# A mixture-of-experts kernel on one core: every expert's split weights get a place of their own in SBUF

## The reference

```python
x = x + jnp.tanh(g_xattn[0]) * _L0_xattn_ref(_layernorm(x), ctx_2048, ...)   # 16 heads of 8 channels, 8 sequences
x = x + jnp.tanh(g_ffn[0]) * _L0_ffn_ref(_layernorm(x), ...)
...
# _L0_ffn_ref: H = 256, M = 176, E = 32 experts, TOPK = 6, 1024 tokens
scores = jax.nn.sigmoid(xf @ w_router)
sfc = scores + corr_bias                       # 4 of 8 groups by their two best, then 6 experts of those
topk_w = jnp.take_along_axis(scores, topk_idx, axis=1)
combine = jnp.zeros((T, E)).at[jnp.arange(T)[:, None], topk_idx].add(topk_w)
eo = jnp.einsum('etm,emh->eth', jax.nn.silu(g) * u, down_w)                   # g, u: xf by gate_w, up_w
routed = jnp.einsum('te,eth->th', combine, eo)
shared = jax.nn.silu(xf @ sh_gate_w) * (xf @ sh_up_w) @ sh_down_w
return routed + shared
```

## Time and profile before

| | |
|---|---|
| median of three runs | 479.46 us |
| profiled execution: span from first to last instruction (no other time is listed for it) | 481.2 us |
| attention and splitting of weights | 0 to about 261 us |
| shared expert, dispatch of rows, table and padding | about 261 to 311 us |
| 79 blocks | about 311 to 463 us |
| sums and output | about 463 to 481 us |
| PE busy | 385.2 us, 80% |
| DVE busy | 353.6 us, 73% |
| ACT busy | 286.4 us, 60% |
| GpSimd busy | 208.0 us, 43% |
| moved by DMA | 101.63 MB, mean 211 GB/s |

### The profile page before, as it was taken

How to read it: one execution, slowest core, us unless ns; L and a number is a source line. 1 busy time by engine, 2 the same in 40 slices (tenths; PEclk the granted TensorE clock), 3 DMA queues, 4 the chain that set the end, 5 groups by cost and what they waited for, 6 DMA issues and landing times.

```text
span 481.2 us, 11851 instructions
## 1 busy us (share of the span) xinstructions
PE 385.2 (80%) x3518; PEld 252.4 (52%) x3518; DVE 353.6 (73%) x998; ACT 286.4 (60%) x538; POOL 208.0 (43%) x368
## 2 busy tenths in 40 slices
PE   0546487987969696958767768899999999999994
PEld 0423244443525253523433445578888888888873
DVE  8157676879998999999746674467777777677784
ACT  1362768687868777865653412366666666666620
POOL 3530102322363656454344650036666566665650
PEclk9996779797979889986857689999999999999999
DMA  7997336563856747676403797577998896545496
GB/s 204 313 308 103 102 101 196 184 206 122 250 170 218 253 154 253 191 238 222 161 29 114 232 311 263 165 238 238 299 287 277 289 291 207 163 151 162 152 378 251
DMA packets 79614, 101.63 MB, mean 211 GB/s; under 512 B 13824, under 2 KB 67808, under 8 KB 79552
## 3 DMA queue, kind: packets, MB, share of 16 engines
q1 hardware_dynamic: 59744, 67.17, 45.1%
q10 hardware_dynamic: 13712, 15.47, 10.6%
q0 software_dynamic: 6096, 18.23, 10.3%
HBM read 56.74 MB, written 44.09 MB: 210 GB/s over the span
## 4 chain that ended last, share of the span: by engine, by line
PE 55%; DVE 24%; DMA 5%; ACT 5%; issue 5%; SPq 2%; ACTq 2%; POOL 0%; PEldq 0%; DVEq 0%; POOLq 0%
PE ps L1183 13%; DVE wide L1287 9%; PE ps L1095 9%; PE ps L990 6%; PE ps L994 5%; DMA ctxb<-picked_rows 4%; PE ps L1165 3%; PE ps L973 3%; DVE rD L1295 3%; DVE pk L1371 3%; PE ps L1087 2%; PE ps L1088 2%; PE ps L930 1%; PE ps L1001 1%; PE ps L959 1%
## 5 line engine op out<-in xcount | busy, mean ns | idle before, releaser
L1287 DVE TENSOR_REDUCE wide<-ps 128x4 f32<-128x1024 f32 x64 | 76.2, 1222 | 24.9 <-PE ps L959 23.9
L690 ACT ACTIVATE wide<-ps 128x1024 f32<-128x1024 f32 x64 | 64.7, 1025 | 36.9 <-PE ps L973 36.4
L1183 PE MATMUL ps<-wide,bxT 128*128 x474 | 83.6, 313 | 0.5 <-ACT bxT L868 0.5
L640 POOL DMA_INDIRECT picked_rows<-by,bid x79 | 77.9, 986 | 12.9 <-POOL tick L639 12.6
L1508 DVE SCALAR_TENSOR_TENSOR bh<-ps,bx,bsg 128x176 f32<-128x176 f32 (+1 forms) x158 | 47.2, 338 | 42.5 <-ACT bsg L884 41.2
L868 ACT ACTIVATE bxT<-ps 128x512 f16<-128x512 f16 x79 | 47.2, 597 | 30.9 <-PE ps L1165 15.6
L1095 PE MATMUL ps<-wide,bhT 112*128 (+1 forms) x395 | 56.5, 272 | 0.3 <-DVE bhT L1517 0.2
L591 POOL DMA_INDIRECT rows_by_expert<-pay,place x48 | 48.4, 1009 | 12.2 <-issue 11.4
L1183 PEld LDWEIGHTS ps<-wide,bxT 128*128 128x128 f16 x474 | 43.1, 98 | 17.0 <-issue 0.8
L990 PE MATMUL ps<-wide 128*32 128x256 f32 x512 | 48.5, 457 | 0.0
L994 PE MATMUL ps<-wide,onesM 128*32 128x256 f32 x512 | 47.0, 444 | 0.0
(11 more groups left out here) (217 smaller groups left out, 738.5 us busy)
## 6 DMA issues: line engine op xcount, KB each, us to landing
bx<-rows_by_expert ACTq DMA_DIRECT2D x72, 160.0 KB
split_weights<-pk SPq DMA_DIRECT2D x26, 352.0 KB, 2.3
wide<-split_weights SPq DMA_DIRECT2D x26, 352.0 KB
raw<-in_L_ffn_gate_w SPq DMA_DIRECT2D x32, 176.0 KB, 2.9
raw<-in_L_ffn_up_w SPq DMA_DIRECT2D x32, 176.0 KB, 2.9
split_weights<-pk SPq DMA_DIRECT2D x26, 192.0 KB, 2.7
wide<-split_weights SPq DMA_DIRECT2D x26, 192.0 KB
rows_by_expert<-filling SPq DMA_DIRECT2D x1, 4960.0 KB, 15.7
```

The source lines that it names most:

```text
L640: nc.gpsimd.indirect_dma_start(PICKED, bass.IndirectOffsetOnAxis(ap=bid[:, j:j + 1], axis=0), by[:, j, :], None).then_inc(placed[j], 16)
L690: act.activation(Pb[:, u % NP, :, :, :], ring(f"B{u}").rearrange("p (i s t) -> p i s t", i=2, s=KT), ACT.Exp, scale=SCALE).then_inc(emptie ...
L1183: last = pe.matmul(ps[:, buf, 0:2 * M], bxT[:, buf, a, k, :], ring_w[:, bass.ds(given[u] + (2 * k + w) * 2 * M, 2 * M)], start=(n == 0), s ...
L1287: dve.tensor_reduce(nmx[:, :, J, 2 * pair:2 * pair + 2, ROW].rearrange("p c g -> p g c"), ring(f"A{u}").rearrange("p (i c s) -> p i c s", ...
```

## The change

- `wide` becomes one room of 32 places, and expert e lies at place e (`all_w`). The ring and its loop are gone. The room of places 9 and up is shared with tiles of the earlier stages: places 9 to 17 with `raw`, `ctxb`, `qk32` and others that are used until the weights are split, 18 to 28 with the heads' tiles, 29 to 31 with those that hold a sequence's rows until they are sent.
- `HELD` is 9: three more experts are never stored or fetched.
- SP fetches each of the other 23 experts in one DMA of 544 KB (L458 of the change). It waits for the expert two before it, by one semaphore for even and one for odd numbers. Experts 9 to 17 wait for the shared expert's split (`w_lo`), 18 to 28 for the end of attention (`p_used`, as 6 to 11 before), and 29 to 31 come after SP's padding.
- The memset of `full` to -1 goes, so an expert without rows has no block. That makes 64 blocks before the fillers, and 15 fillers.
- SP fetches the rows of the first 72 blocks. ACT fetches the last seven.
- The eight parts of the end all lie in `wide`.

The diff, cut:

```diff
-WR = 16
-HELD = 6
-HELD_FIRST = 12
+HELD = 9
+SP_FETCHES = 72
...
+        wide = sb("wide", [128, NE * WX // 2])
+        all_w = wide[:, :].bitcast(F16)
+        with_context = (("raw", RAW * EACH_RAW), ("ctxb", (B + 1) * T), ("xnb", 2 * T), ("qk32", 2 * T), ...
+        with_heads = (("Pb", NP * NG * T), ("qS", NJ * T), ...
+        with_rows = (("rD", T), ("ob", T), ("wT", 4 * 128), ("wo_t", T), ...
+        room, at = {}, HELD * WX // 2
+        free_from = []
+        for group in (with_context, with_heads, with_rows):
+            for name, size in group:
+                room[name] = wide[:, at:at + size]
+                at += size
+            free_from.append(at * 2 // WX)
...
+        parts = [wide[:, six * i:six * (i + 1)] for i in range(B)]
...
+            for par in range(2):
+                sp.sem_inc(weights_in[par], 16 * ((HELD + 1 - par) // 2 + par))
+                sp.wait_ge(stored[par], 32 * ((NE + 1 - par) // 2 - (HELD + 1 - par) // 2))
+
+            def fetch_experts(start, end):
+
+                for e in range(start, end):
+                    sp.wait_ge(weights_in[e % 2], 16 * ((e + 1) // 2))
+                    sp.dma_start(all_w[:, WX * e:WX * (e + 1)], PACK[e]).then_inc(weights_in[e % 2], 16)
+
+            sp.wait_ge(w_lo, 2 * (NE + 2))
+            fetch_experts(HELD, free_from[0])
             sp.wait_ge(p_used, 4 * B)
-            for e in range(HELD, HELD_FIRST):
-                fetch_expert(e, e)
+            fetch_experts(free_from[0], free_from[1])
             sp.wait_ge(tb_step, 1)
             ...
+            sp.wait_ge(pay_step, 3 * B)
+            sp.wait_ge(xT_lo, B)
+            fetch_experts(free_from[1], NE)
             sp.wait_ge(table_ready, 1)
             rows_sent(sp)
-            for b in range(WB - 1):
+            for b in range(SP_FETCHES):
                 row = entry(mybir.EngineType.SP, row_of, b, SPARE + 128 * (SPARES - 1))
-                sp.dma_start(bx[:, b, :], XS[bass.ds(row, 128)]).then_inc(bx_in[b], 16)
-            for e in range(HELD_FIRST, WR):
-                fetch_expert(e, e)
-            with sp.Fori(0, NE // WR - 1) as t:
...
+                if b >= WB:
+                    sp.wait_ge(bid_done, b - WB + 1)
+                sp.dma_start(bx[:, b % WB, :], XS[bass.ds(row, 128)]).then_inc(bx_in[b % WB], 16)
...
-            dve.memset(full[:, :, 0], -1.0)
...
-                dve.tensor_scalar(blocks_to[:, :], tb[0:1, 1, :], 1.0, None, ALU.add)
...
+            dve.tensor_scalar(odd_16[:, :], expert, 16.0, 16.0, ALU.mult, ALU.add).then_inc(odd_step, 1)
+            dve.tensor_scalar(even_of[:, :], even, 16.0, None, ALU.add)
             dve.tensor_copy(row_of[:, :], row)
+            dve.tensor_scalar(place_of[:, 2:130], expert, float(WX), None, ALU.mult)
+            dve.wait_ge(odd_step, 1)
+            dve.tensor_tensor(odd_of[:, :], odd_16[:, :], even, ALU.subtract)
```

More of the change, by code:

```diff
@@ L130, in build @@
[L130 to L136, removed]
@@ new lines, in build @@
+        for group in (with_context, with_heads, with_rows):
[3 more added lines that the diff above has]
+            free_from.append(at * 2 // WX)
+        assert at <= NE * WX // 2
+        raw = room["raw"]
+        ctxb = room["ctxb"].rearrange("p (b t) -> p b t", b=B + 1)
+        xnb = room["xnb"].rearrange("p (a t) -> p a t", a=2)
+        qk32 = room["qk32"].rearrange("p (a t) -> p a t", a=2)
+        qkh, qkl = (room[name].bitcast(F16).rearrange("p (a t) -> p a t", a=2) for name in ("qkh", "qkl"))
@@ new lines, in build @@
+        wnat, wT, onesM = (room[name].rearrange("p (a t) -> p a t", a=4) for name in ("wnat", "wT", "onesM"))
+        ctxv, rD, ob, wo_t, squares, xc, xn2 = (room[name] for name in ("ctxv", "rD", "ob", "wo_t", "squares", "xc", "xn2"))
+        v32, xT32 = (room[name].rearrange("p (k c) -> p k c", k=KT) for name in ("v32", "xT32"))
+        kB = room["kB"].bitcast(F16).rearrange("p (j t) -> p j t", j=NJ)
+        Pb = room["Pb"].rearrange("p (n i s t) -> p n i s t", n=NP, i=2, s=KT)
+        qS, kS, q2S = (room[name].bitcast(F16).rearrange("p (a j t) -> p a j t", a=2, j=NJ) for name in ("qS", "kS", "q2S"))
@@ L204, in split_of @@
             if kind * 4 + i < HELD:
-                whole = ring_w[:, WX * r:WX * (r + 1)]
+                whole = all_w[:, WX * r:WX * (r + 1)]
             else:
@@ L214, in build @@
         six = TOPK * T
-        parts = [raw[:, six * i:six * (i + 1)] for i in range(3)]
-        parts += [pk[:, :, :].rearrange("p b w -> p (b w)").bitcast(F32)[:, 0:six],
-                  wide[:, 0:six], xT_room[:, 0:six], wide[:, six:2 * six], ctxb[:, :, :].rearrange("p b t -> p (b t)")[:, 0:six]]
+        parts = [wide[:, six * i:six * (i + 1)] for i in range(B)]
         bx = sb("bx", [128, WB, PAY])
@@ L861, in keep_xT @@
                     return
-                loads = act.value_load(loads_of[0:1, bass.ds(b, 1)], min_val=16, max_val=16 * NE)
-                act.wait_ge(experts_in, loads)
-                act.wait_ge(downs_in, loads)
+                even = act.value_load(even_of[0:1, bass.ds(b, 1)], min_val=16, max_val=16 * NE // 2)
+                odd = act.value_load(odd_of[0:1, bass.ds(b, 1)], min_val=16, max_val=16 * NE // 2 + 16)
+                act.wait_ge(weights_in[0], even)
+                act.wait_ge(weights_in[1], odd)
                 act.wait_ge(bxT_filled, b + 1)
@@ L1197, in step @@
                     down_products(ps[:, 4 + buf, 0:T], bhT[:, buf, :, :, :],
-                                  lambda rows, w: ring_w[rows, bass.ds(given[u - 2] + (WW + w * T), T)], True, True)\
+                                  lambda rows, w: all_w[rows, bass.ds(given[u - 2] + (WW + w * T), T)], True, True)\
                         .then_inc(by_filled, 1)
@@ L1490, in _ @@
             dve.wait_ge(table_filled, 1)
-            row, weights, expert = (ps[0:1, RANK_BANK, 128 * k:128 * k + 128] for k in range(3))
-            dve.tensor_scalar(loads_of[:, :], expert, 1.0, 16.0, ALU.add, ALU.mult)
+            row, even, expert = (ps[0:1, RANK_BANK, 128 * k:128 * k + 128] for k in range(3))
+            dve.tensor_scalar(odd_16[:, :], expert, 16.0, 16.0, ALU.mult, ALU.add).then_inc(odd_step, 1)
+            dve.tensor_scalar(even_of[:, :], even, 16.0, None, ALU.add)
             dve.tensor_copy(row_of[:, :], row)
-            dve.tensor_copy(place_of[:, 2:130], weights)
+            dve.tensor_scalar(place_of[:, 2:130], expert, float(WX), None, ALU.mult)
+            dve.wait_ge(odd_step, 1)
+            dve.tensor_tensor(odd_of[:, :], odd_16[:, :], even, ALU.subtract)
             dve.tensor_copy(placed_to[:, :], before_end[:, :, 10])
```

87 lines of the change are left out of this document (31 added, 56 removed).

## The result

The changed kernel is slower: 492.26 us (median of 5 runs, 488.51 to 492.91) against 478.23 us of the kernel before on the same chip, a ratio of 1.0262 (95% interval 1.023 to 1.0294). 476.8 us was forecast. On a second chip it took 490.11 us (6 runs) against 479.07, 1.0233 (1.0197 to 1.0269).

The account below looks back on a forecast made before the run. The prediction took PE to bound the blocks at 1.89 us each and the readback to bound the end. Its terms, -4.0 + 1.3 = -2.7 us, gave 476.8 us from a median of 479.46, range 474.5 to 480.0.

Parts of the forecast that it names:

- Fewer blocks before the fillers: End: 64 blocks instead of 71 let the readback start 13.2 us earlier, so PE's waits for parts go, -4.0 us.
- Fetches before the padding: SP's queue before the blocks: 18 landings at 2.1 us each, so padding starts at about 284.7 instead of 280.25.
- with one under way: Expert fetches before the change: 3.6 us per expert, taken as upper bound per landing, 1.8 us if a second doubles the rate.
- Three fetches between padding and rows: SP's queue: fetches of experts 29 to 31 ahead of the rows cost 0 us, with some 5 us in hand.
- Later padding slowing ACT: Before the first block: 4.5 us more of SP's padding slow two more ACT loads by 0.68 us each, +1.3 us.
- The table loads on ACT stay two per block at about 0.28 us: Blocks: ACT loses 72 DMA issues, its loads stay the same, and PE does not wait for ACT, 0 us.
- PE's 20.00 of 20.00 us: Block stage: PE busy throughout, read as no wait to remove; cited against the rival of quicker blocks.
- The rows are late: Rival, start of blocks: above 2.43 us per landing each 0.1 us costs 1.8 us, up to 496 us; chance 0.23.
- 477.5 us at 2.5 us: Late-rows rival: the low end of its time, 477.5 to 480.4 us for landings of 2.5 to 2.7 us.
- the DMA engines are far from full: Argument against the late-rows rival, beside each fetch now waiting for its own predecessor.

Follow-up runs that it names:

- before_no_empty: The kernel before without the line that counts a block for each empty expert, so 64 blocks precede the fillers instead of 71: 477.78 us, ratio 0.9958.
- after_again: The changed kernel itself run once more, with a second profile: 490.11 us, ratio 1.0233.
- lean: The changed kernel with one checked load instead of two on ACT in each block, both semaphores waited for with one number: 487.76 us, ratio 1.0159.
- one_fetch: The changed kernel with one fetch of split weights under way at a time instead of two: 521.53 us, ratio 1.0874.
- last_three: The changed kernel with SP's fetches of experts 29 to 31 moved behind the first eight row fetches: 486.32 us, ratio 1.0158.
- before_two_checked: The kernel before with a second checked load of the same table entry on ACT in each block: 516.53 us, ratio 1.0765.
- both: The changed kernel with early row fetches on SP (experts 18 to 31 fetched between them) and one checked load per block on ACT: 474.68 us, ratio 0.9903.
- rows_first: The changed kernel with SP's padding and row fetches right after experts 9 to 17, experts 18 to 31 fetched between row fetches: 479.83 us, ratio 1.0009.

## Why the prediction was wrong

Its sum was -4.0 + 1.3 = -2.7 us. Measured against before it is about -4.5 at the end, +6 in the blocks and, from 62.9 to the 69.3 and 71.0 us of the changed kernel's two profiles, +6 to +8 at the start: +8 to +10 in all. The medians differ by 14.0 and 11.0 us; on the first chip the profiled execution was the fastest, and where the others lose more was not seen.

- **Fewer blocks before the fillers: right.** -4.0 us forecast; 22.5 to 17.9 us in the profiles, 4.1 us between two runs on one chip. It did not foresee that early parts can delay the last rows, which took 1.5 us of the gain in the profile of before_no_empty.
- **"Fetches before the padding": the step that failed at the start.** It took 2.1 us per landing between 1.8 and 3.6. Measured are 2.65, 2.80 and 2.83 us (the profiles of the changed kernel, after_again and lean). Its reasoning was that two fetches would take whatever sends left of 353 GB/s. But they do not, even where sends are few: from 245 to 257 us, with four sends among them, the DMA engines were busy 0.75 at 256 GB/s and the fetches still took 5.0 us (4.2 and 4.7 in the same stretch of after_again and lean), 2.1 to 2.5 us per landing where 1.8 was taken:

```profile
wide<-split_weights SPq DMA_DIRECT2D x6, 544.0 KB, 5.0
```

  Its 3.6 us "with one under way" were misread. Before, an expert comes as two DMAs, and those ran side by side (SP's timeline of before):

```profile
260.68 0.42 SPq L458 DMA_DIRECT2D wide<-split_weights  x1
263.56 0.32 SPq L456 DMA_DIRECT2D wide<-split_weights  x1
264.47 0.32 SPq L458 DMA_DIRECT2D wide<-split_weights  x1
```

  The second gate-up part goes out at 263.56, as the first has landed, and the first down part is under way until 264.47. So 3.6 us was a pace with two DMAs under way already, and halving it to 1.8 us counted part of the overlap twice. A single DMA of 544 KB at a time has a pace of 4.2 us (one_fetch), two have 2.65 to 2.83: the rate gained is one half. An estimate from the Trainium skill (SBUF — State Buffer, "The DMA setup-cost knee"), with the fixed times of two fetches overlapping, is 1.64 us per landing; the trace disagrees, 2.65, and for one alone 3.3 us against 3.7.
- **"Three fetches between padding and rows": 0 us with 5 us in hand** was true only with padding in time. Once it was late, they cost about 3 us (last_three).
- **Later padding slowing ACT, +1.3 us: not seen.** ACT's loads from the padding table have medians of 852 and 978 ns in the changed kernel's two profiles, against 1096 in the earlier trace rows and 894 to 1136 in the runs with before's order. Its last paddings go out at 298.54 and 296.57, against 301.43 before and 296.75 in before_no_empty. Two pairs beside SP's padding are slower (1.32 and 1.58 us), but the start was set by the rows, so this is off the path.
- **"The table loads on ACT stay two per block at about 0.28 us ... PE does not wait for ACT: 0 us": the step that failed in the blocks.** The count was right and the kind was not read. One `row_of` load of 0.28 us without bounds was exchanged for one of 0.45 to 0.5 us, placed where `bxT` waits behind it, and lean shows about 5 us for it. Nor did PE's 20.00 of 20.00 us say how much room ACT had: it was busy 13.55 us there, with queue instructions not counted, and by before_two_checked it had some 0.2 us per block (an estimate). In the listing of the order the bounds stand as "ISA x2" behind a load.
- **The rivals.** "The rows are late" had the right mechanism. Its limit was 2.43 us per landing and 1.8 us per 0.1 us beyond, on top of 475.5 us; at 2.80 that gives 475.5 + 18 x 0.37 = 482.2 us. (By the same sum its 477.5 us at 2.5 us should be 476.8.) With the 6 us of the blocks it is 488.2, and after_again took 490.1. It got 0.23 of the chance because "the DMA engines are far from full", which the trace of before could not tell about two fetches. No rival held a slower block.

What stays open: why two fetches reach 1.5 times the rate of one; why only some of the 72 blocks without a row fetch are long, and whether the bounds or the place of the load makes them so; why the start of one kernel varies by 2 us between executions; and why the last rows are late beside the parts in lean and both but not in the changed kernel.

## What to carry to other kernels

In this kernel, bringing transfers earlier was harmless only as long as nothing that others wait for stood behind them in the same queue. So count the issues that a late item is moved past, and price a landing with as many under way as there will be. A register load with bounds was three instructions in a row here, so count an engine's queue instructions with its busy time before saying that it has room. Where the measured change is a sum of a gain and two losses, undoing the parts one by one gave a version that is faster than both kernels: here the first rows ahead of the fetches, and one checked load per block, 474.68 us.

## What the runs showed of the hardware

- A load of one table entry into a register of ACT, with bounds, takes 0.45 us in its rows, and a second one cost 0.48 us per block on average where ACT was the loop (before_two_checked). The Trainium skill (DMA: Bandwidth & Descriptors, "Latency and other measured facts") puts the floor of a `tensor_load` at about 600 ns. The trace disagrees: the loads themselves took 277 to 285 ns (medians) in the blocks, and 852 ns beside padding.
- TensorE's granted clock fell while PE waited for rows: 1.00 at 300 us, then 0.60 and 0.50 (1.2 of 2.4 GHz), with no matmul from 308 to 312 us. The first gate-up took 1.94 us for its six matmuls and the second 1.59, where the third took 1.06. Before, this stretch had 1.00. The matmuls of the first two gate-ups thus took 1.4 us longer (1.94 + 1.59 - 2 x 1.06); the first four steps together took 1.1 us more than before's. Late rows are not the whole condition: in rows_first, whose rows are on time, the clock also fell to 0.61 from 308 to 312 us, and its first two gate-ups took 1.58 and 1.97 us; in the run both it stayed at 1.00. What sets those two apart was not tried.

```profile
300.00:304.00 4.00, 2.90 (x23) 2.26 (x24) 2.47 (x10) 1.79 (x6) 0.00 (x0) 1.00 1.07 388
308.00:312.00 4.00, 0.00 (x0) 0.00 (x0) 0.24 (x1) 0.00 (x0) 0.00 (x0) 0.60 0.77 248
312.00:316.00 4.00, 1.32 (x9) 0.88 (x10) 0.00 (x0) 0.60 (x1) 0.00 (x0) 0.50 0.79 251
316.00:320.00 4.00, 4.00 (x24) 2.61 (x24) 0.65 (x3) 1.91 (x5) 0.00 (x0) 0.62 0.49 145
```

These are the busy times by stretch of the changed kernel; the third number from the end is the clock.
